# Batch 3's two low parts, moved from VectorE to GpSimd, in a fused int8 layer and top-2 expert FFN

## What is computed

```python
def _smooth_quant_linear(x, w):
    s = jnp.sqrt(jnp.maximum(amax_x, EPS) / jnp.maximum(amax_w, EPS))
    ...
    return x_q @ w_q.T * x_scale * w_scale.T

def _L0_ffn_ref(hidden_states, gate_w, w1, b1, w2, b2):
    x = hidden_states.reshape(-1, d)
    router_logits = x @ gate_w.T
    _, sel = jax.lax.top_k(router_logits.sum(axis=0), TOP_K)
    rw = jax.nn.softmax(router_logits[:, sel].astype(jnp.float32), axis=1)
    h = jax.nn.gelu(jnp.einsum('nd,kdf->knf', x, w1[sel]) + b1[sel][:, None, :])
    y = jnp.einsum('knf,kfd->knd', h, w2[sel]) + b2[sel][:, None, :]
    out = jnp.einsum('nk,knd->nd', rw, y)
    ...
x = x + _L0_xattn_ref(_layernorm(x, axis=-1), fside_BxS2xS2_0, ctx_1024)
x = x + _L0_ffn_ref(_layernorm(x, axis=-1), gate_w, w1, b1, w2, b2)
```

## Time and profile before

| | |
|---|---|
| median of 3 runs | 824.86 us (823.83 to 825.81) |
| the profiled execution's own time | 823.26 us |
| its span, first to last instruction | 821.4 us |
| PE busy | 775.2 us, 94% |
| VectorE busy | 487.6 us, 59% |
| GpSimd busy | 445.9 us, 54% |
| ScalarE busy | 355.2 us, 43% |
| mean granted clock of PE | 0.976 of 2.4 GHz |

### The profile page before, as it was taken

One profiled execution on the slowest core, in us unless ns is written; L12 is line 12 of the kernel. 1 busy time (PEld: TensorE's weight loads), 2 busy tenths in 40 slices (PEclk: granted clock), 3 DMA queues, 4 the chain that ended last, 5 costly groups with the idle time before them and its releaser, 6 DMA issues.

```text
span 821.4 us, 11341 instructions
## 1 busy us (share of the span) xinstructions
PE 775.2 (94%) x3570; PEld 624.4 (76%) x3577; DVE 487.6 (59%) x693; ACT 355.2 (43%) x660; POOL 445.9 (54%) x473
## 2 busy tenths in 40 slices
PE   5778866999999999999999999999999999999998
PEld 4656543688788888888888888888888888888886
DVE  6999979797754545454545454545454545454545
ACT  3958687733442424242424242424242424242422
POOL 1678898158564646464646464646464646464622
PEclk9799986999999999999999999999999999999999
DMA  9400000301000000000101010101010101000022
GB/s 345 171 1 1 1 1 1 128 1 36 17 27 25 28 24 28 23 28 23 28 23 29 22 30 21 31 20 29 22 32 19 30 21 31 20 31 20 0 103 102
DMA packets 19077, 32.33 MB, mean 39 GB/s; under 512 B 872, under 2 KB 11240, under 8 KB 18160
## 3 DMA queue, kind: packets, MB, share of 16 engines
q1 hardware_dynamic: 18896, 31.98, 11.3%
q10 hardware_dynamic: 160, 0.08, 0.0%
HBM read 27.87 MB, written 4.19 MB: 39 GB/s over the span
## 4 chain that ended last, share of the span: by engine, by line
PE 82%; DVE 9%; POOL 4%; issue 3%; DMA 1%; ACT 1%; ACTq 0%; DVEq 0%; POOLq 0%
PE slot L781 42%; PE slot L768 34%; PE slot L826 3%; DVE rmax L1192 2%; DVE xf L1249 1%; DVE peak_x L1192 1%; POOL res L373 1%; DVE peak_a L1192 1%; DVE xf L1260 1%; DMA b_rows<-in_L_ffn_b 1%; POOL cv L348 1%; DVE stats L1183 1%; POOL rstd L333 1%; POOL h_lo L450 1%; PE slot L563 1%
## 5 line engine op out<-in xcount | busy, mean ns | idle before, releaser
L768 PE MATMUL slot<-xo,a_hi 128*128 128x512 f32 x840 | 259.0, 389 | 0.0
L1513 DVE SCALAR_TENSOR_TENSOR res<-slot,rw,res 128x512 f32<-128x512 f32 x256 | 178.5, 751 | 130.3 <-PE slot L781 130.2
L1542 DVE TENSOR_TENSOR e<-slot,e 128x512 f32<-128x512 f32 x150 | 103.8, 692 | 173.4 <-PE slot L768 173.3
L781 PE MATMUL slot<-w_hi,h_hi 128*128 128x512 f32 x512 | 201.0, 393 | 0.4 <-POOL h_lo L450 0.4
L781 PE MATMUL slot<-w_lo,h_hi 128*128 128x512 f32 x512 | 199.4, 389 | 0.0
L781 PE MATMUL slot<-w_hi,h_lo 128*128 128x512 f32 x512 | 199.3, 389 | 0.0
L768 PEld LDWEIGHTS slot<-xo,a_hi 128*128 128x128 f32 x840 | 157.3, 188 | 33.4 <-DVE e L1542 0.2
L450 POOL TENSOR_TENSOR h_lo<-e,h_hi 128x512 fp32r<-128x512 f32 x96 | 138.2, 1453 | 55.3 <-ACT e L1070 54.3
L768 PE MATMUL slot<-xo,a_lo 128*128 128x512 f32 x420 | 163.4, 389 | 0.0
L781 PEld LDWEIGHTS slot<-w_hi,h_hi 128*128 128x128 f32 x512 | 96.1, 188 | 25.2 <-POOL h_lo L450 5.6
L781 PEld LDWEIGHTS slot<-w_hi,h_lo 128*128 128x128 f32 x512 | 96.1, 188 | 20.2
(11 more groups left out here) (145 smaller groups left out, 825.3 us busy)
## 6 DMA issues: line engine op xcount, KB each, us to landing
raw<-in_L_ffn_w SPq DMA_DIRECT2D x32, 512.0 KB, 3.4
res<-in_x SPq DMA_DIRECT2D x4, 1024.0 KB, 11.8
wv<-in_fside_BxS2xS SPq DMA_DIRECT2D x4, 1024.0 KB, 12.7
out_x<-res SPq DMA_DIRECT2D x3, 1024.0 KB, 3.9
cv<-in_ctx SPq DMA_DIRECT2D x4, 512.0 KB, 13.0
out_x<-res SPq DMA_DIRECT2D x4, 256.0 KB, 2.7
b_row<-in_L_ffn_b SPq DMA_DIRECT2D x2, 256.0 KB, 4.6
b_rows<-in_L_ffn_b ACTq DMA_DIRECT2D x1, 64.0 KB, 5.8
```

Of the source, the lines that this page charges most:

```text
L768: last = t.matmul(dst, a[:, i, k, :], xo[tp][:, v, k, :], start=(start and n == 0), stop=(n == 3 * H - 1), skip_group_check=True)
L781: last = t.matmul(y_bank[j][:, :], a[:, i, j * P:(j + 1) * P], v[:, f, :], start=(start and n == 0), stop=(not start and n == 2), skip_gro ...
L1513: v.scalar_tensor_tensor(out=r, in0=y_bank[j][:, :], scalar=rw[:, ds(p, 1), n:n + 1].rearrange("p a b -> p (a b)"), in1=r, op0=ALU.mult, o ...
L1542: v.tensor_tensor(dst[:, :], src, other[:, :], ALU.add).then_inc(comb_ready, 1)
```

## The change

VectorE no longer calls `keep_lo(3, 0)` and `keep_lo(3, 1)`. GpSimd makes the same two subtractions, on the same buffers and with the same semaphores, behind `inv_std(3, 2)`, through a new function `batch_lo`.

```diff
@@ -377,6 +377,12 @@
+
+            def batch_lo(b, h):
+                pool.wait_ge(hi_ready[b], h + 1)
+                tp, n = b // 2, b % 2
+                g.tensor_tensor(whole(tp, LO_AT[n][h]), part(tp, FULL_AT[n][h]),
+                                whole(tp, HI_AT[n][h]).bitcast(F32), ALU.subtract).then_inc(lo_ready[b], 1)
@@ -442,6 +448,8 @@
             inv_std(2, 2)
             normalise(2)
             inv_std(3, 2)
+            batch_lo(3, 0)
+            batch_lo(3, 1)
 
             pool.sem_inc(sums_ready, 4)
@@ -1478,8 +1486,6 @@
             choose_experts()
             pick_experts()
             keep_lo(2, 1)
-            keep_lo(3, 0)
-            keep_lo(3, 1)
             first_weights()
```

## The result

Over 21 runs of each, the changed kernel takes 827.25 us (825.28 to 829.94) and the kernel before 825.34 us (821.90 to 827.24). The ratio is 1.0027, with a 95% interval from 1.0018 to 1.0036: slower by 2.2 us (1.5 to 3.0) by the ratio, by 1.9 us by the medians.

The account below looks back on a forecast made before the run. PE, busy 94% of the span, was taken as the bound, its first FFN matmul's start deciding: 2.52 us delay less 0.39 us slack is +2.1 us, 824.86 + 2.1 = 827.0 us; range 826.0 to 828.0.

Parts of the forecast that it names:

- PE is saturated behind 162 us: From 162 to 820 us PE is busy 654.92 of 658.00 us, so an earlier delay remains at the end.
- GpSimd takes 2.43 us for 128x1024: Length of each moved subtraction on GpSimd, extended from its smaller rows; 2.40 us taken from start to start.
- The second low part 2.52 us later: Batch 3's second low part ends at 157.14 us instead of 154.62; less 0.39 us slack, first FFN matmul +2.1 us.
- Removing VectorE's work gains nothing: Taking 2.33 us of subtractions off VectorE before 154.62 us saves nothing; its next work waits for ScalarE's `a_hi`.
- The first `a_lo` late, but covered: VectorE's first `a_lo` is ready near 157.56 us at worst; L826 needs it at 158.15 us, 0.6 us of cover.
- The second rival: VectorE's four `a_lo` hold up GpSimd's second subtraction by 1.43 us, giving 828.4 us; chance 0.05.
- The third rival: Not slower: shift under 1.65 us, an instruction under 2.17 us; 826.0 us at about 1.9 us each; chance 0.16.
- The first rival: PE's clock falls in the gap around batch 3's router, 1.7 us lost, 828.7 us; chance 0.19.
- A fall between 154 and 162 us: Sign of being wrong: PE's granted clock falls around batch 3's router and the first FFN matmuls.
- the main case: GpSimd's subtractions delay the first FFN matmul by +2.1 us without a further effect, 827.0 us; chance 0.57.

Follow-up runs that it names:

- the first trace: First profiled execution of the changed kernel (both low parts on GpSimd): 13.79 us from A to C, PE's clock at half for 3.4 us.
- PE kept busy: Changed kernel plus 5 unused matmuls of the router's shape ahead of each half of batch 3's router: 826.43 us, ratio 1.0019 against the kernel before.
- the fourth execution: Another profiled execution of the unaltered changed kernel, clock at full: 6.81 us from A to B, 12.38 us from A to C.

## Why the prediction was right, point by point

- **PE is saturated behind 162 us, so a delay there stays.** Right. From C to the end it is 659.7 us before and after, and 659.6 to 659.9 us in the other traces.
- **GpSimd takes 2.43 us for 128x1024, 2.40 from start to start.** Right within 0.07 us: 2.37 us, and 4.69 us for both. The step from 128x256 to 128x512 carried further gives it.
- **The second low part 2.52 us later, less 0.39 us of slack, +2.1 us.** Right. It ends 2.38 us later in the first trace and 2.45 with PE kept busy; the slack is 0.42 us; B moves by 1.96 us in the fourth execution, where the clock stayed, and by 2.01 with PE kept busy.
- **Removing VectorE's work gains nothing.** Right: it idles 3.17 us for `a_hi`.
- **The first `a_lo` late, but covered.** Right. It ended 0.28 us after GpSimd (154.66 + 1.78 = 156.44 us), and PE took it up more than a microsecond later. The first gelu and GpSimd's next work kept their cover too.
- **The second rival, a collision the other way,** did not occur: GpSimd's second instruction showed 2.37 us with VectorE waiting for it. In the kernels with three subtractions and VectorE's `a_lo` due while GpSimd ran, the last one took up to 2.59 us, 0.2 us over.
- **The third rival, a shift too small to be told,** failed on its condition: 2.37 us an instruction is over the 2.17 us named.
- **The first rival, the fall of PE's clock, was underrated.** A fall between 154 and 162 us was one of the prediction's own signs of being wrong, and it came: the clock was at half from about 155.9 to 159.3 us in the first trace. I gave it 0.19, with the argument that the low share of PE would stand for a short stretch only. It came in 4 of 5 profiled executions. Its price, 1.7 us, was near the 1.4 us measured. So the profile mostly looked like the rival, while the time came out at the main case's. The main case's mechanism is shown where the clock stayed; that +2.1 us also meets the 2.2 us timed is in part luck, since the sum has no term for the falls.
- **Why the time is nearer the main case is not settled.** The pure delay of 1.9 us and 1.4 us in 4 of 5 executions would make 3.0 us; the two timings gave 2.2 (1.5 to 3.0) and 2.6 us (1.2 to 3.9). The first interval just reaches it. In which of the timed executions the clock fell can't be seen, but each has its mean granted clock on record, and 2 x (1 - clock) x span is its time at half clock. That is 36.7 us on the mean of 33 executions of the changed kernel and 35.6 us of 75 of the kernel before: 1.0 us more, with a standard error of 0.7. A fall in every execution would add 3.4 us, in 4 of 5 2.7 us. So an estimate is a fall in 3 of 10, and 1.9 + 0.3 x 1.4 = 2.3 us, near both timings. That points to the fall being rarer than the five profiles have it, and does not show it: the clocks are rounded to 0.001, which is 1.6 us, and the kernel with only the second part moved has 3.2 us more at half clock than before (standard error 1.3), with no fall here in its trace. The spread of A, several microseconds between traces of the same code, is larger than the difference, and was not taken apart.

## What to carry to other kernels

An engine's idle stretch is worth nothing when what is moved into it lies on the chain and takes twice as long there: price the moved step by the receiving engine's row, and count it from when its input is ready, not from when the engine fell idle. Subtract the slack of the consumer, which is found by asking what else it waits for; here 0.4 us of a 2.4 us delay. And when a wait of PE grows, look at what share of that stretch it would be busy: the delay can bring half-clock matmuls behind it, which unused matmuls in the wait took away again here.

## What the runs showed of the hardware

- The clock of PE fell without any idle gap over 1.33 us: in the changed kernel it had been busy 1.14 of the 3.40 us before the fall, between gaps of 1.33 and 1.14 us, and the second was still open when the clock fell. In another execution it was busy 1.13 of 3.60 us in the same place and did not fall. The same code behaves both ways.
- Adding 20 unused matmuls made the kernel with three subtractions faster, 828.87 against 832.68 us; its trace keeps the full clock where the other's is at half for 6 us.
- VectorE's instruction with two inputs in SBUF, started while GpSimd's ran, ended 1.07 us after GpSimd's, although it needs 1.23 us alone; its start is not lost entirely. GpSimd's own length did not grow (2.37 us). With four of VectorE's `a_lo` due beside three subtractions of GpSimd, GpSimd's last one took 2.51 and 2.59 us.
